# Moving value, feature, down and Wo·U steps in a hand-written order of an attention block with generated weights

## The reference

```python
h = x + relu(x @ w_down[b]) @ w_up[b]          # w_down, w_up from the condition
paths = sigmoid(h @ Wp + bp)                   # 8 heads, depth 5
agree = pq * pk + (1 - pq) * (1 - pk)
sim = cumprod(agree).sum() / DEPTH             # causal, then softmax over the keys
x = x + (softmax(sim) @ (h @ Wv)) @ Wo
z = x @ U[b];  y = z @ V + bias                # U[b]: 257 x 30, from the condition
e = argmax(y @ gate_w.T)                       # 8 experts
out = x + y + y @ expert_w[e]
```

## Time and profile before

| | us |
|---|---|
| median of 3 runs | 156.72 |
| lowest and highest run | 153.45, 157.16 |
| the profiled execution's own time | 153.24 |
| its span (first to last instruction) | 151.5 |
| PE busy | 135.7 (90%) |
| DVE busy | 98.8 (65%) |
| ACT busy | 56.2 (37%) |
| POOL busy | 48.6 (32%) |

### The profile page before, as it was taken

How to read it: one execution, slowest core, us unless ns; L and a number is a source line. 1 busy time by engine, 2 the same in 40 slices (tenths; PEclk the granted TensorE clock), 3 DMA queues, 4 the chain that set the end, 5 groups by cost and what they waited for, 6 DMA issues and landing times.

```text
span 151.5 us, 4920 instructions
## 1 busy us (share of the span) xinstructions
PE 135.7 (90%) x2182; PEld 85.1 (56%) x2182; DVE 98.8 (65%) x183; ACT 56.2 (37%) x67; POOL 48.6 (32%) x71
## 2 busy tenths in 40 slices
PE   5989679999779879994999999949999998999993
PEld 5655455553445566562655765536558675666651
DVE  0673628848988758837937579188376967985431
ACT  3013460565053406545422461481334457310010
POOL 7200074032055460560056444600645652110000
PEclk9999999999999999999999999999999999999999
DMA  4989899600112000000000100000101000011211
GB/s 110 330 366 456 362 373 352 248 12 0 16 23 32 0 4 4 0 4 0 35 17 22 43 4 35 4 0 0 39 35 39 4 35 6 35 37 37 71 37 69
DMA packets 7381, 12.49 MB, mean 82 GB/s; under 512 B 1552, under 2 KB 5808, under 8 KB 7232
## 3 DMA queue, kind: packets, MB, share of 16 engines
q1 hardware_dynamic: 7120, 11.73, 21.7%
q0 software_dynamic: 96, 0.05, 1.1%
q10 hardware_dynamic: 144, 0.39, 0.7%
HBM read 9.95 MB, written 2.22 MB: 80 GB/s over the span
## 4 chain that ended last, share of the span: by engine, by line
PE 67%; DVE 21%; issue 5%; POOL 3%; ACT 2%; DVEq 0%; POOLq 0%; ACTq 0%
PE work L636 36%; PE c_ps L636 15%; PE s_ps L636 11%; DVE tiles L576 4%; DVE tiles L579 3%; PE work L760 2%; DVE rden L476 2%; DVE feat L626 2%; POOL zo L406 2%; DVE h_t L509 1%; DVE logit L519 1%; ACT prob L423 1%; ACT v_sb L431 1%; PE work L820 1%; PE work L812 1%
## 5 line engine op out<-in xcount | busy, mean ns | idle before, releaser
L423 ACT ACTIVATE prob<-s_ps 128x1536 f32<-128x1536 f32 (+1 forms) x24 | 38.2, 1593 | 40.8 <-PE s_ps L636 40.8
L387 POOL TENSOR_SCALAR_AFFINE_SELECT prob<-prob 128x1024 f32<-128x1024 f32 x16 | 18.4, 1152 | 74.3 <-ACT prob L423 74.2
L476 DVE RECIPROCAL rden<-c_ps 128x256 f32<-128x256 f32 x16 | 28.1, 1757 | 8.5 <-PE c_ps L636 8.4
L636 PE MATMUL s_ps<-phi_t 32*128 32x256 f32 (+1 forms) x384 | 24.2, 365 | 1.1 <-DVE phi_t L526 0.6
L636 PEld LDWEIGHTS s_ps<-phi_t 32*128 32x128 f32 x384 | 17.4, 184 | 11.6 <-issue 9.0
L636 PE MATMUL c_ps<-prob,v_sb 128*32 128x256 f32 (+1 forms) x384 | 22.1, 347 | 0.0
L399 POOL TENSOR_TENSOR short<-prob 128x512 f32<-128x512 f32 x15 | 19.3, 1289 | 1.2
L636 PE MATMUL work<-ctx_t,mix_sb 128*32 128x256 f32 x256 | 17.0, 381 | 0.4
L636 PE MATMUL work<-zo_t,gexp 128*32 128x256 f32 x256 | 16.9, 379 | 0.0
L636 PEld LDWEIGHTS c_ps<-prob,v_sb 128*32 128x32 f32 x384 | 10.9, 109 | 9.0 <-issue 3.1
L636 PE MATMUL work<-w_vl,h_t 128*32 128x296 f32 x208 | 15.1, 415 | 0.4 <-DVE h_t L509 0.4
(11 more groups left out here) (102 smaller groups left out, 155.8 us busy)
## 6 DMA issues: line engine op xcount, KB each, us to landing
wdec<-in_W_dec SPq DMA_DIRECT2D x1, 3855.0 KB, 18.3
x_t<-in_x_tr SPq DMA_DIRECT2D x4, 512.0 KB, 8.4
ex_t<-in_expert_tr SPq DMA_DIRECT2D x1, 2048.0 KB, 25.0
out_x<-x_t SPq DMA_DIRECT2D x16, 128.0 KB, 1.7
mix_sb<-in_mix SPq DMA_DIRECT2D x1, 776.0 KB, 19.6
lift_sb<-in_lift ACTq DMA_DIRECT2D x1, 384.0 KB, 4.0
w_vl<-in_vl SPq DMA_DIRECT2D x1, 296.0 KB, 5.2
first_sb<-in_first SPq DMA_DIRECT2D x1, 144.0 KB, 3.8
```

The lines of the kernel that those rows point to most:

```text
L387: nc.gpsimd.affine_select(out=tri, in_=tri, compare_op=ALU.is_ge, fill=0.0, base=0, pattern=[[0, HG], [0, 2], [1, P]], channel_multiplier= ...
L423: nc.scalar.activation(prob[:, p % 2, :, 0:width(p)], s_ps[:, :, 0:width(p)], ACT.Exp).then_inc(exped, 1)
L476: link(nc.vector.reciprocal(rden[:], c_ps[m % 2][:, CW:2 * CW]))
L636: return nc.tensor.matmul(o, w, r, start=start, stop=stop, skip_group_check=True)
```

## The change

It moves steps in the list and changes nothing that they compute. For batch 1's features: `feat` leaves the place behind `tanh` and stands in the next gap, ahead of that gap's contexts and behind `add`; the same for batches 2 and 3. `Q` moves from gap 3 to gap 4 of batch 0, behind `ubT`. `down 2` moves ahead of `G 1`, and `down 3` ahead of an output step. `WoU` moves ahead of both up steps of batch 2. The value steps of batches 2 and 3 move up one place each: the first to behind `zT`. The output step `(out, 0, 3)` moves from behind context 13 to behind `tanh` of batch 3. Since the banks are taken in turn, several steps change bank.

```diff
 def features(b, ts):
-    return [("bias", b, ts), ("tanh", b, ts), ("feat", b, ts)]
+    return [("bias", b, ts), ("tanh", b, ts)]
...
 # PROLOGUE: ("feat", 0, FIRST) now written out at the same place
...
 # after_scores
     if n1 < B:
+        gaps[0] += [("WoU",)] if b == 1 else []
         gaps[0] += [("up", n1, 0), ("up", n1, 1)]
+        gaps[3] += [("feat", n1, ALL_T)]
         gaps[4] += [("phi", n1, 0, ALL_T), ("phi", n1, 1, ALL_T)]
...
     elif n1 < B:
-        gaps[0] += [("WoU",)] if b == 1 else []
-        gaps[1] += [("zs", prv, ALL_T), ("zo", prv, 0), ("zo", prv, 1), ("VL", n1, 0)]
-        gaps[2] += [("VL", n1, 2)]
+        gaps[1] += [("zs", prv, ALL_T), ("zo", prv, 0), ("zo", prv, 1), ("VL", n1, 1)]
+        gaps[2] += [("VL", n1, 3)]
...
 # after_context, b == 0
-        gaps[3] += [("Q",), ("gup", n2)]
-        gaps[4] += [("G", 0), ("ubT",)]
-        gaps[5] += [("G", 1), ("down", n2)]
+        gaps[3] += [("gup", n2)]
+        gaps[4] += [("G", 0), ("ubT",), ("Q",)]
+        gaps[5] += [("down", n2), ("G", 1)]
     else:
         gaps[0] += [("zT", prv, ALL_T)]
         gaps[3] += [("out", prv, 0)]
         gaps[4] += [("out", prv, 1)]
+        gaps[5] += [("down", n2)] if n2 < B else []
         gaps[5] += [("out", prv, 2)]
-    if prv >= 1:
+    if b >= 1 and n1 < B:
+        gaps[0] += [("VL", n1, 0)]
+        gaps[1] += [("VL", n1, 2)]
+        gaps[2] += features(n1, ALL_T)
+        gaps[2] += [("out", prv - 1, 3)] if prv >= 1 else []
+    elif prv >= 1:
         gaps[1] += [("out", prv - 1, 3)]
-    if b >= 1 and n1 < B:
-        gaps[1] += [("VL", n1, 1)]
-        gaps[2] += [("VL", n1, 3), *features(n1, ALL_T)]
-    if b >= 1 and n2 < B:
-        gaps[5] += [("down", n2)]
```

More of the change, by code:

```diff
@@ L105, in features @@
 def features(b, ts):
-    return [("bias", b, ts), ("tanh", b, ts), ("feat", b, ts)]
+    return [("bias", b, ts), ("tanh", b, ts)]
 PROLOGUE = [("gdn", (0,)), ("gup", 0), ("down", 0), ("gdn", (1, 2, 3)), ("up", 0, 0), ("up", 0, 1), ("gup", 1),
-            ("VL", 0, 0), ("VL", 0, 1), *features(0, FIRST), ("VL", 0, 2), ("VL", 0, 3), ("bias", 0, SECOND),
+            ("VL", 0, 0), ("VL", 0, 1), *features(0, FIRST), ("feat", 0, FIRST), ("VL", 0, 2), ("VL", 0, 3), ("bias", 0, SECOND),
             ("phi", 0, 0, FIRST), ("phi", 0, 1, FIRST), ("tanh", 0, SECOND), ("scores", 0), ("feat", 0, SECOND),
```

## The result

| | before | changed |
|---|---|---|
| median of 4 runs | 155.08 us | 151.62 us |
| lowest, highest | 153.09, 157.16 | 151.52, 154.99 |
| span of the profiled execution | 151.5 | 149.8 |
| its own time | 153.24 | 151.52 |
| its mean granted TensorE clock | 1.000 | 0.988 |

The account below looks back on a forecast made before the run. PE is busy 90% of a 151.5 us span, so only its idle time can be won. The terms -0.30 + 1.46 + 0.97 + 1.88 = 4.01 take 153.24 to 149.2 us; range 146.7 to 152.7.

Parts of the forecast that it names:

- second rival: Features leave the adds but stand ahead of the division: gain only 1.9 us, so 151.3; chance 0.23.
- D: Batch 2's second half: denominators' wait goes, 0.1 stays for the zoT copy; gain 1.88 us, at least 0.6.
- A: Batch 0 up to scores 6: Q waits for G's addition; loss of 0.30 us, bounds +0.8 and -1.1.
- signs of being wrong: PE idling ahead of WoU, the first wait moving to the next DVE row at 1.3, or batch 3's attention changing length.
- B: Turn to batch 2: waits of 0.69 and 0.77 us both go; gain 1.46, at least 1.0.
- C: Batch 1's second half: 0.62 of the denominators' 1.98 us wait stays, phi's second half waits 0.70; gain 0.97.
- slower rival: WoU waits for u_w and all of batch 2 behind it, making the kernel slower; chance 0.08 including the unseen.

Follow-up runs that it names:

- experiment 1: The changed kernel plus eight unit matmuls on TensorE ahead of the second half of batch 1's phi transposes; median 150.23 us, ratio 0.979.
- experiment 4: The kernel before with only batch 1's features moved behind the sum of key tiles; 152.58 to 152.91 us at clock 1.000, ratio 0.997.
- experiment 5: The kernel before plus unit matmuls (5, 8 and 8) in its three waits for the sum of key tiles; 152.91 to 154.26 us.
- experiment 6: The changed kernel with gup 2 before context 3, five unit matmuls before ubT, G 1 before context 5, WoU behind context 6; 149.12 to 149.52 us.
- experiment 7: The kernel of experiment 2 with G 1 ahead of context 5 and WoU behind context 6, without fillers; median 151.07 us, ratio 0.986.
- experiment 9: The kernel of experiment 6 with WoU copied out by ScalarE instead of VectorE; median 148.62 us, ratio 0.970.
- experiment 10: The kernel of experiment 9 without the five unit matmuls ahead of ubT; median 149.94 us, ratio 0.979.
- experiment 8: The changed kernel with batch 1's features, Q, gup 2, G, down 2 and WoU put back as before; 150.01 to 150.96 us, ratio 0.981.
- experiment 3: The changed kernel with gup 2 moved ahead of context 3; 149.67 and 149.74 us at clock 1.000, 150.64 and 150.75 at 0.989.
- experiment 2: The changed kernel with batch 1's features alone put back ahead of the adds; median 150.27 us, ratio 0.980.

## Why the prediction was wrong

The direction held, the size did not: 1.7 of 4.0. The prediction had given 0.62 to a gain of over 2% and 0.30 to one within it. That the time of 151.6 lies inside the range is luck: the range reached that far for another reason, an execution like the median. The second rival's 151.3 is close by luck too: it took 1.3 from D, which gained nearly what was forecast, and its 0.8 in A was not for the clock.

- **The step that failed is A.** Its working put scores 6 at 46.07, from the chain of VectorE's steps and Q's bank wait. That chain was right: the second `phi` half at 42.80 (42.5 forecast, and the start-up was 0.34 later), Q waiting 0.34 for G's addition, and with the clock kept, 0.31 lost against 0.30. What was left out is what idle time does to the clock. The prediction said that all costs are waits; but the idle time hardly grew, to 2.35 (2.01 and 0.34) from 2.13, and the matmuls behind it became slower. A came out at -1.77, below its lower bound of -1.1, and 1.46 of that is the fall of the clock (experiment 1). One of the prediction's own signs of being wrong had come: the first wait moved whole to a later row of VectorE, `w_up`. The prediction even said that 1.31 would be freed and soon met by the next wait, and did not ask what that does to the clock with the idle time in one piece where there had been 1.31, 0.57 and 0.25. The trace before gave no warning, with full clock behind two spells of 1.98; that was one execution, and experiments 4 and 5 point at these spells for the falls in others. The spread of the three runs, 153.45 to 157.16, was the sign of it, and I took it for a shift of all executions.
- **B was mis-sized: +0.91, not +1.46,** and below its own floor of 1.0. Both waits went, but the cover failed. I took the first up half as 0.57, half of the pair's 1.14. In the changed kernel the pair takes 1.75, and VectorE's first `h_t` starts 1.17 after the pair does, so the first half alone takes about as long as both together; the second, held back by `WoU`'s copy, adds what is left. That is 0.61 more than 1.14, where B lacks 0.55. The row of VectorE:

```profile
55.79 1.31 DVE L511 TENSOR_TENSOR h_t<-work,x_t 128x512 f32<-128x512 f32 x2 [0.60 <-PE work L638]
```

Experiments 6, 7, 9 and 10, with `WoU` out of the way, have 1.14 again. The Trainium skill states, in TensorEngine Tiling (Array Packing), section Key Properties, that different tiles of the array can run their loads and matmuls in parallel. The two halves have 64 rows each, and the rows agree: 1.14 for both together, 1.75 apart.
- **C was right in its parts:** +1.15 for +0.97. The denominators waited 0.37 (0.62 forecast), `phi`'s second half 0.53 for L616's addition (0.70). VectorE's rows show the two delays beside POOL's mask and addition that the sum contained, bias 0.95 instead of 0.66, the first add 1.80 instead of 0.68:

```profile
66.94 0.95 DVE L521 TENSOR_TENSOR logit<-v_sb,bp_b 128x160 f32<-128x160 f32 x1 [0.36 <-ACT v_sb L433]
67.81 1.80 DVE L578 TENSOR_TENSOR tiles<-tiles,prob 128x512 f32<-128x512 f32 x1
```

- **D was right in size and cause:** +1.77 for +1.88, with no wait ahead of the denominators and 0.23 for ACT's `zoT` copy.
- **The rivals.** Features did come back as a late division, but cost no more than was in the sum. `WoU` never waited for `u_w`; the slower rival had no part in it. The start-up, whose matmuls the change leaves in their order, was 0.34 later in this execution; over the traces of all twelve kernels scores 4 start at 34.44 to 35.45.
- **The change as a whole** is two changes. Its later half is worth 3 us (experiment 8). Its earlier half takes about 1.5 of that back, nearly all of it by one fall of the clock. With the clock kept, the earlier half is worth nothing that the medians show (150.23 in experiment 1, 150.10 in experiment 8).

Of the fall, the condition remains open. 2.01 of idle brought it in all four runs of the changed kernel, to go by their mean clocks; 1.26 brought it in two of four in experiment 3 and in all six in 10; 1.30 or 1.31 at another place brought none in the 13 runs of experiments 2, 7 and 8. So the length of a spell alone does not decide. What caused the further falls of the changed kernel's run at 0.967 isn't shown.

One fall cost 1.46 in experiment 1, 1.0 in 3 and 1.3 in 10. The levels of the kernel before are further apart at first, 153.2 to 155.8 and then 157.1, and no trace shows why.

The Trainium skill, TensorE: Matmul & The Clock Gate, section A second HAM failure mode: psum-queue depth-cycling, tells of a bf16 kernel that goes through PSUM banks in turn, in which frequent short idle spells between groups of matmuls let the clock swing between its two levels. The same swing is seen in this fp32 kernel, but here a single idle spell was followed by it (2.01 in the changed kernel, 1.26 in experiment 3).

## What to carry to other kernels

Idle time on TensorE is not priced by its sum: a reordering that gathers small waits into one can cost more than it saves, so ask of every move which idle pieces it joins, and look at the granted clock behind them, in more than one execution. Runs of one kernel at separate levels, here 153.2, 155.8 and 157.1, can be a finding and not noise; compare their mean clocks before the medians. Where a wait can't be removed, a few matmuls into a bank that is overwritten anyway kept the clock in every run here, and they make a clean experiment too, since nothing else moves.

## What the hardware showed that I had not expected

- One idle spell of 2.01 us was followed by 0.50 of the clock for over 3 us, at a cost of 1.46 us; one of 1.26 by 0.50 as well, at 1.0 (experiment 3) and 1.3 (experiments 9 and 10). One of 1.30 or 1.31 elsewhere in the order was not, in 13 runs.
- Two matmul groups on different 64-row halves of the array take 1.14 us issued together and 1.75 with a wait of VectorE's between them.
- The levels of the kernel before vanish with 21 matmuls in three waits: ten runs at 1.000, where it had eight of 14.
